# Decoder layer on one core: four row-maxima tiles and one norm step of the third attention change their place in a hand-written order

## The chip, the cores and the metric

The kernel runs on one core of a Trainium2 chip as one launch. The metric is the device time of that launch in microseconds. Before the change the median of 3 runs is 3247.62 us (3247.37 to 3250.29).

## The reference, cut to what matters

A post-norm decoder layer on x (16 x 224 x 512) and a context (16 x 750 x 512), in four parts one after the other: a causal self-attention with low-rank additions to its weights, a second self-attention with biases, a cross-attention of 224 queries on 750 keys per batch, and a feed-forward part (512 to 2048 to 512, then a second one with ternary weights). Each attention has 16 heads of 32. The change touches the third one:

```
Q = split(q_in @ wq + bq, Sq)
K = split(k_in @ wk + bk, Sk)
V = split(v_in @ wv + bv, Sk)
scores = jnp.einsum('bhqd,bhkd->bhqk', Q, K) / HD ** 0.5
probs = jax.nn.softmax(scores, axis=-1)
ctx = jnp.einsum('bhqk,bhkd->bhqd', probs, V)
...
x = _ln(x + h, ln2_g, ln2_b)
```

## The kernel before, in words

Every matmul of the attentions is done in float16 halves (a high and a low part of each operand), so that one product of the reference becomes three. The work of an attention is cut into **units**: one batch and one group of four heads, so four units a batch (g = 0 to 3, called first to fourth unit here) and 64 units an attention. A unit of the cross-attention has these steps; their letters are those of the order tables.

- **q, k0, k1, v0, v1**: projections (L769 on PE). Each ends in one of two banks of PSUM (`ps_proj`). ACT writes the high half (L937, L933), DVE the low half (L981, L979), and with that the bank is free. k0, k1 and v0 are issued on PE in two halves, k0a and k0b and so on; ACT and DVE act after the second.
- **spill, stack**: SP sends the projected Q and K to memory and back into the layout of the scores.
- **M0 to M7, the maxima tiles**: eight per unit (four heads, two tiles of 128 queries). For one tile PE computes 128 x 750 scores with two matmuls of 375 columns (L855), and DVE reduces them to a row maximum (L988, `at_mx_cross`). There is one buffer for such a tile, `ps_qk`, two banks wide, so PE waits before each tile until DVE has reduced the one before it (L851, quoted below).
- **row**: the unit's 8 maxima are transposed on PE (L826), rescaled on ACT (L925, `at_mrow`) and laid by SP as one more row under the queries, so that the scores come out with the maximum already taken off.
- **S0 to S11, the scores**: transposed scores for a pair of key chunks (L890, two matmuls of 224 columns). ACT computes the exponential twice, once to float16 (L944) and once in place (L945), and DVE subtracts the one from the other for the low half (L997, the subtraction). Three banks go round, so PE's Sn waits for the subtraction of S(n-3).
- **V0 to V11, the values**: probabilities times values (L911, eight short matmuls); Vn waits for the subtraction of Sn.
- **E0, E1**: the two evacuations of the values' sums (L951 on ACT; after E1 a reciprocal on DVE, L1002, and two steps on POOL).

At a batch's end come **norm** (L1010, L1014 on DVE, then POOL, L1098 and L1100), **apply** (two DVE operations of 128x512, L1036, then two on POOL, L1106 and L1109) and **store**.

The wait of PE before a maxima tile, in `Attention.tensor`:

```
if self.cross or n == 0 and g == 0 and b == self.b0:
    wait(pe, self.max_done, self.tile(b, g, n))
```

What sets the order is a table written by hand, `ORDERS` (from L58), with one line of tokens for each of the four units of a batch. The function `step` (L1713) turns a line into events, and every engine walks through the same list of events, taking from each what is its own part. So the table fixes the order of each engine's queue, and an engine never takes a later event first. Not every token is of the unit in whose line it stands. With the last tuple of the table, (3, 2, 1, 2), projections, spill and stack in unit u are those of unit u+3, maxima tiles those of unit u+2 (`MAX_AHEAD`), row is that of u+1, and the scores S0 and S1 are those of u+1, while S2 to S11 and all V are of u itself. E1 in unit u is that of u-1. `norm` and `apply` are those of the batch before. The tokens x0, x1, c0 to c5, splitx, splitc, load, loadc, residual, spill, stack and store have no part on PE, ACT or DVE in this attention.

The unit's own work on the three engines is about the same for all four, save that the second unit also has norm and apply.

## Time and profile before

| | |
|---|---|
| median of 3 runs | 3247.62 us |
| profiled execution, its time | 3245.53 us |
| profiled execution, its span | 3243.7 us |
| granted TensorE clock, mean | 0.978 |
| causal attention and second self-attention | up to about 1180 us of the span |
| cross-attention | about 1180 to 2370 us |
| feed-forward part | from about 2370 us |
| busy share of the span | PE 92%, PEld 73%, DVE 79%, ACT 62%, POOL 42% |

PE is the matmul part of TensorE and PEld its weight loads, which run beside the matmuls. DVE is VectorE, ACT ScalarE, POOL GpSimd, SP the queue that issues most transfers. A line such as L855 is a line of the kernel. In a timeline, "x2" counts instructions that were merged, and a bracket at the end gives the idle time before a row and what ended it. The matmuls' ends are modelled; two rows of PE are best compared by their starts.

### The profile page before, as it was taken

To read this page: it belongs to the slowest core of one execution; us is meant where nothing else is said; L and a number is where in the kernel's file an instruction comes from. 1 tells how busy PE (TensorE), PEld (TensorE's weight loads), DVE (VectorE), ACT (ScalarE), POOL (GpSimd) and SP (SyncE) were. 2 spreads that over 40 slices of the span, in tenths; PEclk is the share of its full clock that TensorE was granted. 3 is DMA by queue.
4 is the path that set the end of the run, shared out by engine and by line. 5 is a ranking of instruction groups with operands and counts; after the bars stand their busy time and mean duration, and the time that the engine had idled before them with its cause. 6 is when DMAs were issued, how large, how long until landed. Compare 5 with 4: busy or idle time off the path is not lost.

```text
span 3243.7 us, 87025 instructions
## 1 busy us (share of the span) xinstructions
PE 2988.8 (92%) x34642; PEld 2369.2 (73%) x34642; DVE 2567.3 (79%) x4750; ACT 1995.7 (62%) x4650; POOL 1349.9 (42%) x1273
## 2 busy tenths in 40 slices
PE   7998999988999769999999999999889999999996
PEld 4987888888899647777877778877765565565662
DVE  4776888888899669999999999999846666666666
ACT  2655565667787537777777777877655445344352
POOL 0675632257765544444344344443132232222232
PEclk9999999999999889999999999999899999999997
DMA  4666655456554546655655555554341121211212
GB/s 127 185 206 223 194 180 153 135 159 202 174 162 140 150 118 134 141 141 125 140 137 134 137 135 147 134 129 106 125 152 40 46 53 53 56 45 44 56 40 49
DMA packets 430834, 405.86 MB, mean 125 GB/s; under 512 B 272368, under 2 KB 346240, under 8 KB 429280
## 3 DMA queue, kind: packets, MB, share of 16 engines
q1 hardware_dynamic: 415600, 348.64, 41.0%
q0 software_dynamic: 14576, 51.40, 5.1%
q8 instruction: 277, 4.54, 0.6%
q14 instruction: 125, 1.02, 0.1%
q10 hardware_dynamic: 256, 0.26, 0.0%
HBM read 239.98 MB, written 109.52 MB: 108 GB/s over the span
## 4 chain that ended last, share of the span: by engine, by line
PE 51%; DVE 18%; DMA 13%; ACT 8%; issue 4%; SPq 4%; POOL 1%; ACTq 0%; DVEq 0%; POOLq 0%
PE at_ps L769 22%; PE at_ps L1430 4%; PE at_ps L911 4%; PE at_ps L855 4%; DVE at_mx_cross L988 4%; DVE at_p L997 3%; DMA self_spill<-at_proj 3%; PE at_ps L1444 3%; PE at_ps L890 3%; PE at_ps L1455 3%; PE at_ps L1411 2%; ACT at_ps L945 2%; DVE at_proj L981 2%; DMA at_o_raw<-at_values 2%; PE at_ps L865 2%
## 5 line engine op out<-in xcount | busy, mean ns | idle before, releaser
L944 ACT ACTIVATE at_p<-at_ps 125x448 f16<-125x448 f32 (+2 forms) x1280 | 676.9, 529 | 285.9 <-PE at_ps L890 196.5
L997 DVE TENSOR_TENSOR at_p<-at_ps,at_p 125x448 f16<-125x448 f32 (+2 forms) x1280 | 750.5, 596 | 129.3 <-ACT at_ps L945 119.3
L945 ACT ACTIVATE at_ps<-at_ps 125x448 f32<-125x448 f32 (+2 forms) x1280 | 679.5, 531 | 0.0
L988 DVE TENSOR_REDUCE at_mx_cross<-at_ps 128x1 f32<-128x750 f32 x512 | 476.7, 931 | 26.9 <-PE at_ps L855 24.5
L1070 POOL TENSOR_TENSOR at_o_sum<-at_o_raw 128x256 f32<-128x256 f32 x192 | 121.2, 631 | 782.6 <-ACT at_o_raw L951 782.1
L911 PE MATMUL at_ps<-at_values,at_p 112*128 112x65 f16 (+3 forms) x6656 | 303.3, 185 | 23.4 <-DVE at_p L997 10.5
L1478 ACT ACTIVATE at_masks<-at_ps,at_b_cols 128x256 f32<-128x256 f32 x224 | 106.7, 476 | 336.2 <-PE at_ps L1411 336.1
L992 DVE TENSOR_REDUCE at_mx<-at_ps 112x2 f32<-112x448 f32 (+1 forms) x512 | 303.9, 609 | 10.0 <-PE at_ps L865 7.0
L1411 PE MATMUL at_ps<-at_xt,at_early 128*128 128x256 f16 x1792 | 302.1, 276 | 8.9 <-ACT at_w_first L1479 6.1
L911 PEld LDWEIGHTS at_ps<-at_values,at_p 112*128 112x128 f16 (+1 forms) x6656 | 267.2, 97 | 49.3 <-ACT at_o_raw L951 19.7
L1430 PE MATMUL at_ps<-at_w_second,at_w_first 128*128 128x512 f16 x896 | 283.6, 379 | 0.0
L769 PE MATMUL at_ps<-at_xt,at_w_first 128*128 128x224 f16 x2304 | 254.1, 262 | 3.6 <-DVE at_xt L979 3.0
L769 PE MATMUL at_ps<-at_w_first,at_masks 128*125 128x128 f16 (+1 forms) x2688 | 240.1, 245 | 0.4 <-DVE at_proj L981 0.4
L769 PEld LDWEIGHTS at_ps<-at_xt,at_w_first 128*128 128x128 f16 x2304 | 216.8, 99 | 7.1 <-DVE at_xt L979 3.4
L890 PE MATMUL at_ps<-at_stacks 97*125 97x224 f16 (+1 forms) x1280 | 208.9, 265 | 6.7 <-DMA at_stacks<-at_mrow 6.1
L769 PEld LDWEIGHTS at_ps<-at_w_first,at_masks 128*125 128x125 f16 (+1 forms) x2688 | 179.7, 132 | 40.4 <-issue 2.8
L865 PE MATMUL at_ps<-at_stacks 96*128 96x224 f16 (+2 forms) x1024 | 177.6, 252 | 32.7 <-DMA at_stacks<-self_spill 26.1
L1411 PEld LDWEIGHTS at_ps<-at_xt,at_early 128*128 128x128 f16 x1792 | 175.8, 99 | 37.4 <-ACT at_w_first L1479 6.8
L1411 PE MATMUL at_ps<-at_xt,at_prep 128*128 128x256 f16 x672 | 184.3, 274 | 0.0
L951 ACT COPY at_o_raw<-at_ps 128x260 f32<-128x260 f32 x384 | 147.7, 385 | 55.3 <-PE at_ps L911 55.3
L890 PEld LDWEIGHTS at_ps<-at_stacks 97*125 97x125 f16 (+1 forms) x1280 | 149.9, 136 | 32.1 <-DMA at_stacks<-at_mrow 9.4
L769 PE MATMUL at_ps<-at_xt,at_w_second 128*128 128x224 f16 x1536 | 169.5, 265 | 0.4 <-DVE at_values L979 0.3
(217 smaller groups left out, 6941.7 us busy)
## 6 DMA issues: line engine op xcount, KB each, us to landing
at_x_res<-x SPq DMA_DIRECT2D x124, 256.0 KB, 3.2
cross_spill<-at_proj SPq DMA_DIRECT2D x64, 487.0 KB, 3.2
at_x_rows<-x SPq DMA_DIRECT2D x92, 256.0 KB, 3.1
at_prep<-bit POOLq DMA_DIRECT2D x32, 512.0 KB, 5.5
at_early<-ctx SPq DMA_DIRECT2D x32, 512.0 KB, 5.3
at_stacks<-cross_spill SPq DMA_DIRECT2D x64, 243.5 KB, 3.7
causal_spill<-at_proj SPq DMA_DIRECT2D x64, 224.0 KB, 3.5
at_stacks<-causal_spill SPq DMA_DIRECT2D x128, 112.0 KB, 2.3
```

Of the source, the lines that this page charges most:

```text
L769: mm = pe.matmul(out, left(i, c), right(j, c), start=c == 0 and n == 0, stop=c == DC - 1 and n == 2)
L865: last = pe.matmul(out[:, t, 0:keys[t]], qs[0:96, n, q0:q0 + rows], ks[0:96, n, 0:keys[t]], start=True, stop=not self.causal)
L890: last = pe.matmul(mem.ps_st[0:KC, bank, at:at + T], ks[:, h, c * KC:(c + 1) * KC], qs[:, h, 0:T], start=True, stop=True)
L911: last = pe.matmul(mem.ps_pv[:, t, at_h:at_h + cols], left, vs[:, c, h, 0:cols], start=n % HALF == 0 and c == 0 and t == 0 and k == 0, sto ...
L944: act.activation(mem.p_hi[0:self.KC, n % 4, 0:self.P_COLS], scores, ACT.Exp, scale=EXP_SCALE)
L945: act.activation(scores, scores, ACT.Exp, scale=EXP_SCALE).then_inc(self.exp_done, 1)
L951: act.copy(mem.o_raw[:, g % 2, :, 2 * VW * n:2 * VW * (n + 1)], mem.ps_pv).then_inc(self.pv_evac, 1)
L988: dve.tensor_reduce(self.mx[:, at, t, h:h + 1], mem.ps_qk[:, :, 0:self.KT // 2], AX.XY, ALU.max).then_inc(self.max_done, 1)
L992: dve.tensor_reduce(self.mx[0:rows, at, :, n], mem.ps_qk[0:rows, n % 2, 0:2 * T].rearrange("p (t k) -> p t k", t=2), AX.X, ALU.max).then_i ...
L997: dve.tensor_tensor(mem.p_lo[0:self.KC, n % 4, cols], mem.ps_st[0:self.KC, self.st_bank(b, g, n), cols], mem.p_hi[0:self.KC, n % 4, cols], ...
L1411: last = pe.matmul(out, self.f1[w][quarter][:, c, at:at + P], self.xt[:, x, c, :], start=c == 0 and k == 0, stop=c == DC - 1 and k == 2)
L1430: last = pe.matmul(mem.ps_c[:, t, :], self.ht[:, x, c, t * P:(t + 1) * P], self.f2[w][:, c, :], start=c == 0 and k == 0, stop=c == FC - 1 ...
```

## The change

Only the cross-attention's table changes, and `step` learns one more letter. `L` is like `M`, a maxima tile, but of the unit `MAX_AHEAD - 1` = 1 ahead, not 2.

- Second unit's line: M6 and M7 are gone. M0 stands behind k1b, no longer ahead of it. M1 stands behind S5 (and x0, x1), no longer between V1 and S5. M5 stands behind S11, no longer ahead of it. apply is gone.
- Third unit's line: L6 stands behind E1 and L7 behind V0; these are the tiles that the second unit gave up. M0 moves from behind q to behind k0a, M1 from ahead of S4 to behind k1a, M2 from there to behind V3, M3 from behind V3 to behind S7, M6 from behind V8 to behind V10. M7 is gone. apply stands behind k0b.
- Fourth unit's line: L7 stands behind S2.

The first unit's line is as before. No instruction is added or taken away; the queue of SP has the same order as before.

```diff
--- before.py
+++ after.py
@@ -69,11 +69,11 @@
                (5, 3, 2, 1)),
     "cross": (("c4 E1 S2 k0a V0 V1 M0 k0b V2 M1 S3 q row M2 S4 V3 k1a M3 residual c5 S5 k1b M4 S6 V4 S7 S8 V5 v0a M5 "
                  "E0 S9 v0b V6 S10 spill V7 load M6 splitx S11 S0 V8 v1 S1 stack V9 M7 V10 V11",
-                 "S2 k0a splitc0 E1 S3 k0b norm S4 V0 q k1a M0 k1b V1 M1 spill S5 apply x0 x1 stack V2 V3 V4 M2 "
-                 "S6 S7 V5 row v0a M3 S8 E0 v0b M4 S9 V6 V7 V8 S10 M5 S11 v1 M6 loadc0 S0 V9 V10 V11 M7 S1",
-                 "E1 q M0 S2 S3 V0 c0 splitc1 k0a M1 S4 c1 k0b k1a M2 S5 V1 k1b row V2 S6 V3 M3 V4 S7 S8 v0a V5 M4 E0 "
-                 "S9 v0b V6 M5 S10 spill S11 V7 v1 V8 M6 S0 V9 stack loadc1 V10 S1 V11 M7",
-                 "E1 S2 S3 q V0 c2 V1 row V2 splitc2 c3 M0 S4 k1a M1 loadc2 S5 k1b M2 S6 S7 V3 V4 V5 k0a E0 M3 S8 k0b "
+                 "S2 k0a splitc0 E1 S3 k0b norm S4 V0 q k1a k1b M0 V1 spill S5 x0 x1 M1 stack V2 V3 V4 M2 "
+                 "S6 S7 V5 row v0a M3 S8 E0 v0b M4 S9 V6 V7 V8 S10 S11 M5 v1 loadc0 S0 V9 V10 V11 S1",
+                 "E1 L6 q S2 S3 V0 L7 c0 splitc1 k0a M0 S4 c1 k0b apply k1a M1 S5 V1 k1b row V2 S6 V3 M2 V4 S7 M3 S8 v0a V5 "
+                 "M4 E0 S9 v0b V6 M5 S10 spill S11 V7 v1 V8 S0 V9 stack loadc1 V10 M6 S1 V11",
+                 "E1 S2 L7 S3 q V0 c2 V1 row V2 splitc2 c3 M0 S4 k1a M1 loadc2 S5 k1b M2 S6 S7 V3 V4 V5 k0a E0 M3 S8 k0b "
                  "M4 S9 V6 v0a M5 S10 S11 V7 V8 V9 spill M6 S0 v0b stack S1 V10 v1 store M7 V11"),
                (3, 2, 1, 2)),
 }
@@ -1728,6 +1728,8 @@
                     at, what = resolve(b, g + (0 if n >= layer.AHEAD else 1)), ("scores", n)
                 elif kind == "V":
                     at, what = (layer, b, g), ("values", n)
+                elif kind == "L":
+                    at, what = resolve(b, g + layer.MAX_AHEAD - 1), ("max", n)
                 elif kind == "M":
                     at, what = resolve(b, g + layer.MAX_AHEAD), ("max", n)
                 elif kind == "E":
@@ -1759,7 +1761,7 @@
                     yield at[0], "stack", at[1], at[2], 0
                     yield None, "prep", 0, 0, turn
                     continue
-                if kind in ("E", "S", "M") or token in ("row", "spill", "stack") or token in at[0].UNIT_JOBS:
+                if kind in ("E", "S", "M", "L") or token in ("row", "spill", "stack") or token in at[0].UNIT_JOBS:
                     yield at[0], what[0], at[1], at[2], what[1]
                 else:
                     yield at[0], what[0], at[1], 0 if kind != "V" else g, what[1]
```

The order of DVE's queue in the second unit of a batch, from the subtraction of S4 on. L981 with 224 columns is q, with 375 a half of the keys; L988 is a maxima tile; L1036 is apply. Before:

```order
L997 TENSOR_TENSOR at_p<-at_ps,at_p 125x448
L981 SCALAR_TENSOR_TENSOR at_proj<-at_ps,at_cross_b_cols,at_proj 128x224
L988 TENSOR_REDUCE at_mx_cross<-at_ps 128x1
L981 SCALAR_TENSOR_TENSOR at_proj<-at_ps,at_cross_b_cols,at_proj 128x375
L988 TENSOR_REDUCE at_mx_cross<-at_ps 128x1
L997 TENSOR_TENSOR at_p<-at_ps,at_p 125x448
L1036 TENSOR_SCALAR at_yn<-at_z,at_mv,at_rstd 128x512 x2
L988 TENSOR_REDUCE at_mx_cross<-at_ps 128x1
L997 TENSOR_TENSOR at_p<-at_ps,at_p 125x448 x2
```

Now:

```order
L997 TENSOR_TENSOR at_p<-at_ps,at_p 125x448
L981 SCALAR_TENSOR_TENSOR at_proj<-at_ps,at_cross_b_cols,at_proj 128x224
L981 SCALAR_TENSOR_TENSOR at_proj<-at_ps,at_cross_b_cols,at_proj 128x375
L988 TENSOR_REDUCE at_mx_cross<-at_ps 128x1
L997 TENSOR_TENSOR at_p<-at_ps,at_p 125x448
L988 TENSOR_REDUCE at_mx_cross<-at_ps 128x1 x2
L997 TENSOR_TENSOR at_p<-at_ps,at_p 125x448 x2
L988 TENSOR_REDUCE at_mx_cross<-at_ps 128x1
```

What moved: the low half of k1 now stands ahead of M0, both M1 and M2 stand behind the subtraction of S5, and apply is gone.

The order of DVE's queue in the third unit, from the subtractions of S2 and S3 on. Before (the first L988 is M1, the last M3):

```order
L997 TENSOR_TENSOR at_p<-at_ps,at_p 125x448 x2
L988 TENSOR_REDUCE at_mx_cross<-at_ps 128x1
L997 TENSOR_TENSOR at_p<-at_ps,at_p 125x448
L981 SCALAR_TENSOR_TENSOR at_proj<-at_ps,at_cross_b_cols,at_proj 128x375
L988 TENSOR_REDUCE at_mx_cross<-at_ps 128x1
L997 TENSOR_TENSOR at_p<-at_ps,at_p 125x448
L981 SCALAR_TENSOR_TENSOR at_proj<-at_ps,at_cross_b_cols,at_proj 128x375
L997 TENSOR_TENSOR at_p<-at_ps,at_p 125x448
L988 TENSOR_REDUCE at_mx_cross<-at_ps 128x1
L997 TENSOR_TENSOR at_p<-at_ps,at_p 125x448 x2
L988 TENSOR_REDUCE at_mx_cross<-at_ps 128x1
```

Now (the two L988 of the second row are L7 and M0, then M1, M2, M3):

```order
L997 TENSOR_TENSOR at_p<-at_ps,at_p 125x448 x2
L988 TENSOR_REDUCE at_mx_cross<-at_ps 128x1 x2
L997 TENSOR_TENSOR at_p<-at_ps,at_p 125x448
L981 SCALAR_TENSOR_TENSOR at_proj<-at_ps,at_cross_b_cols,at_proj 128x375
L1036 TENSOR_SCALAR at_yn<-at_z,at_mv,at_rstd 128x512 x2
L988 TENSOR_REDUCE at_mx_cross<-at_ps 128x1
L997 TENSOR_TENSOR at_p<-at_ps,at_p 125x448
L981 SCALAR_TENSOR_TENSOR at_proj<-at_ps,at_cross_b_cols,at_proj 128x375
L997 TENSOR_TENSOR at_p<-at_ps,at_p 125x448
L988 TENSOR_REDUCE at_mx_cross<-at_ps 128x1
L997 TENSOR_TENSOR at_p<-at_ps,at_p 125x448
L988 TENSOR_REDUCE at_mx_cross<-at_ps 128x1
```

What moved: L7 and M0 stand behind the subtraction of S3, M2 behind that of S6 and M3 behind that of S7, and apply stands ahead of M1.

The order of PE's queue in the third unit, from the last matmul of V0 on. L769 with x6 is a half of k0, with x12 k0b and k1a. Before (the two L855 are M1 and M2):

```order
L911 MATMUL at_ps<-at_values,at_p 128x65
L769 MATMUL at_ps<-at_w_second,at_w_first 128x375 x6
L855 MATMUL at_ps<-at_w_first 128x375 x2
L890 MATMUL at_ps<-at_stacks 125x224 x2
L769 MATMUL at_ps<-at_w_second,at_w_first 128x375 x12
L855 MATMUL at_ps<-at_w_first 128x375 x2
```

Now (the L855 are L7, M0 and M1):

```order
L911 MATMUL at_ps<-at_values,at_p 128x65
L855 MATMUL at_ps<-at_stacks 128x375 x2
L769 MATMUL at_ps<-at_w_second,at_w_first 128x375 x6
L855 MATMUL at_ps<-at_w_first 128x375 x2
L890 MATMUL at_ps<-at_stacks 125x224 x2
L769 MATMUL at_ps<-at_w_second,at_w_first 128x375 x12
L855 MATMUL at_ps<-at_w_first 128x375 x2
```

What moved: L7 and M0 now stand with only one half projection, six matmuls, between them.

## Rows read from the trace of the kernel before

**Rows 1.** Windows, one per unit (second, third, fourth, first); columns: window, length, busy times, clock, DMA.

```profile
1511.16:1531.28 20.12, 17.87 (x253) 14.86 (x249) 18.93 (x34) 14.16 (x32) 6.90 (x6) 1.00 0.66 124
1531.28:1549.07 17.79, 17.41 (x249) 14.75 (x247) 16.09 (x26) 15.14 (x34) 7.78 (x6) 1.00 0.44 111
1549.07:1567.22 18.15, 17.80 (x247) 14.49 (x246) 16.64 (x27) 14.76 (x33) 5.47 (x5) 1.00 0.68 133
1567.22:1585.12 17.90, 17.66 (x252) 14.71 (x249) 15.97 (x26) 13.99 (x33) 12.04 (x9) 1.00 0.70 183
```

**Rows 2.** Line L855 within 1230:2310, its idle time by releaser (us, times).

```profile
  DVE at_mx_cross L988: 111.5, 231
```

**Rows 3.** Timeline of PE, second unit; columns: start us, length us, instruction, idle before.

```profile
1516.01 0.49 PE L855 MATMUL at_ps<-at_stacks 96*128 96x375 f16 x2
1516.34 1.12 PE L769 MATMUL at_ps<-at_w_second,at_w_first 128*128 128x375 f16 x6
1517.30 0.39 PE L911 MATMUL at_ps<-at_prep,at_p 125*128 125x33 f16 x8
1518.28 0.49 PE L855 MATMUL at_ps<-at_stacks 96*128 96x375 f16 x2 [0.59 <-DVE at_mx_cross L988]
...
1519.81 0.49 PE L855 MATMUL at_ps<-at_stacks 96*128 96x375 f16 x2 [0.18 <-DVE at_mx_cross L988]
...
1520.70 0.40 PE L911 MATMUL at_ps<-at_prep,at_p 125*128 125x33 f16 x8
...
1526.88 0.49 PE L855 MATMUL at_ps<-at_stacks 96*128 96x375 f16 x2 [0.87 <-DVE at_mx_cross L988]
...
1530.75 0.50 PE L855 MATMUL at_ps<-at_stacks 96*128 96x375 f16 x2 [0.60 <-DVE at_mx_cross L988]
```

**Rows 4.** Timeline of DVE, second unit.

```profile
1517.29 0.93 DVE L988 TENSOR_REDUCE at_mx_cross<-at_ps 128x1 f32<-128x750 f32 x1
1518.14 0.60 DVE L981 SCALAR_TENSOR_TENSOR at_proj<-at_ps,at_cross_b_cols,at_proj 128x375 f16<-128x375 f32 x1
1518.81 0.94 DVE L988 TENSOR_REDUCE at_mx_cross<-at_ps 128x1 f32<-128x750 f32 x1
1520.02 0.62 DVE L997 TENSOR_TENSOR at_p<-at_ps,at_p 125x448 f16<-125x448 f32 x1 [0.27 <-ACT at_ps L945]
1520.56 0.99 DVE L1036 TENSOR_SCALAR at_yn<-at_z,at_mv,at_rstd 128x512 f32<-128x512 f32 x2
```

**Rows 5.** Timeline of PE, third unit.

```profile
1532.76 0.55 PE L890 MATMUL at_ps<-at_stacks 97*125 97x224 f16 x4
...
1539.11 0.38 PE L890 MATMUL at_ps<-at_stacks 97*125 97x224 f16 x2
1539.33 0.39 PE L911 MATMUL at_ps<-at_values,at_p 125*128 125x65 f16 x8
1539.56 0.48 PE L855 MATMUL at_ps<-at_w_first 96*128 96x375 f16 x2
...
1542.13 0.48 PE L855 MATMUL at_ps<-at_w_first 96*128 96x375 f16 x2
...
1548.74 0.49 PE L855 MATMUL at_ps<-at_w_first 96*128 96x375 f16 x2 [0.33 <-DVE at_mx_cross L988]
```

**Rows 6.** Timeline of DVE, third unit.

```profile
1534.39 1.29 DVE L997 TENSOR_TENSOR at_p<-at_ps,at_p 125x448 f16<-125x448 f32 x2
...
1540.55 0.62 DVE L997 TENSOR_TENSOR at_p<-at_ps,at_p 125x448 f16<-125x448 f32 x1 [0.43 <-ACT at_ps L945]
1541.09 0.93 DVE L988 TENSOR_REDUCE at_mx_cross<-at_ps 128x1 f32<-128x750 f32 x1
```

**Rows 7.** Windows of the second self-attention and of the cross-attention.

```profile
700.00:1180.00 480.00, 419.96 (x5837) 382.51 (x5834) 402.22 (x865) 325.78 (x773) 328.27 (x304) 0.96 0.55 162
1480.00:1780.00 300.00, 287.00 (x3985) 237.88 (x3983) 274.16 (x446) 235.49 (x519) 131.24 (x106) 1.00 0.59 136
```

## The prediction

> **What bounds the kernel now.** I read the windows first, cut at the start of each unit of one batch of the cross-attention [rows 1]. The four lengths add up to 73.96 us a batch. The second unit is the longest, 20.12 us against 17.79 to 18.15, and there DVE is busy for 18.93 us, 94% of it. PE does the same matmuls in every unit, so the extra time is lost on it. Then I read one line, L855, the matmuls of the maxima tiles: over 1080 us its rows had 111.5 us of idle time that a DVE reduction ended (weight loads and matmuls counted apart) [rows 2]. Last the timelines show how. PE's queue is in order, and it stops before a maxima tile until the one before is reduced: in the second unit four times [rows 3]. By starts, less the work between them, it loses 0.76 us at the first (a values pair takes 0.22, so from 1517.30 + 0.22 to 1518.28), 0.17 more than the bracket shows, since ends are modelled. The others so read are 0.35, 1.04 and 0.77, and a values pair waits for 0.16 (1519.81 + 0.33 + 0.40 to 1520.70): 3.08 us. That leaves 17.04 us of work in the unit, and by the same work the third unit lost 0.75, the fourth 1.1 and the first 0.85 [rows 1]. DVE in the second unit has norm and apply besides.
>
> So PE's order is the path of the attention, and a stop of PE counts unless a later stop shrinks by it.
>
> **The prices, from rows.** (a) From the start of a reduction to the next tile on PE: 1517.29 to 1518.28, 0.99 us [rows 3, 4]. (b) From a tile's start on PE to its reduction at the earliest: 1518.28 to 1518.81, 0.53. (c) From scores on PE, over ACT's two exponentials, to the subtraction on DVE at the earliest: 1539.11 to 1540.55, 1.44 [rows 5, 6], and 18.61 to 20.02 gives 1.41 by the next start behind the tile at 1518.28 (0.33 for the tile) [rows 3, 4]; I take 1.41. For two scores in a row the second subtraction starts at 1534.39 + 1.29 - 0.62 = 1535.06 for scores at 1532.76, so 2.30 [rows 5, 6]. (d) A subtraction holds DVE for 0.54 before a reduction may start (1540.55 to 1541.09), a reduction 0.85 (1517.29 to 1518.14, its row says 0.93, so 0.08 overlaps), apply 0.99 less the same 0.08, so 0.91 [rows 4]. (e) The low half of a key projection: 1516.34 to 1518.14, 1.80 from its last half's start. (f) PE: tile 0.33, scores 0.20, values 0.22, half of a key projection 0.96 (1516.34 to 1517.30).
>
> DVE's queue is in order too. A tile whose reduction stands behind a subtraction pays (c), (d) and (a) before PE may start the next tile: 1.41 + 0.54 + 0.99 = 2.94 us from the scores. Before, this happens with long work between: S6 at 1539.11, M3's reduction at 1541.09, M4 at 1542.13, with a half of v0 in between [rows 5, 6].
>
> **Part by part.** No instruction is added or removed, so nothing costs by itself.
>
> *Second unit.* M0 goes behind k1b and starts at 1516.97. On DVE its reduction stands behind k1's low half, ready at 1516.01 + 1.80 = 1517.81, and 0.53 long, so it runs at 1518.34 and M1 may start at 19.33. On PE only V1 and S5 lie between, up to 17.72: a stop of 1.6 us where there was one of 0.76. M1 is reduced at 19.33 + 0.53 = 19.86, so M2 starts at 20.85, 1.04 later than before [rows 3]. Of that the wait of 0.16 at the values pair is taken back; M4 is 0.88 late. M4's reduction stands behind v0's low half as before, so M5 keeps its distance and comes at 27.76 for 26.88. Behind it S11 is already done (0.20), M6 and M7 are gone (0.65) and the stop before M7 (0.77). The unit ends at 30.5 for 31.28: **0.75 us less**, of which 0.65 is work that is done one unit later.
>
> *Third unit, start.* Here PE meets S2, S3, V0, L7, k0a, M0, with L7 and M0 behind the subtraction of S3 on DVE. M0 may start 2.30 + 0.54 + 0.99 = 3.83 us after S2, and PE has 0.40 + 0.22 + 0.33 + 0.96 = 1.91 us of work: at least 1.92 lost in both stops. L6 also stands behind the last subtractions of the unit before and the reciprocal, which makes it some 2.1: L7 starts at 1533.6 and M0 at 36.05.
>
> *Third unit, middle.* From M0 on three halves of key projections lie between the tiles, so apply (0.91 on DVE), between k0's low half and M1, is covered: M2 has its release at 40.8 and comes at 41.05. If that cover went, it would cost up to its 0.91. Then S6, V3, M2, V4, S7, M3: M2's reduction stands behind the subtraction of S6, so M3 can't come before S6 + 2.94, and PE has 0.20 + 0.22 + 0.33 + 0.22 + 0.20 = 1.17 of work: 1.77 lost at least, 2.0 with ACT still busy with S6 (row and k1 are ahead of it). M3 at 43.8, M4 at 45.95. Going on to the unit's end, with M6 behind V10: 52.0 where 49.07 was. In sum 2.1 + 2.0 and a third of a microsecond for one more tile, less the 0.75 that the unit lost before (0.50 of it at 1548.74, bracket and 0.17) [rows 1, 5]: **+3.7**.
>
> *Fourth unit.* S0, V9, V10, M6, S1, V11, S2, L7: M6's reduction is behind the subtraction of S0, so L7 waits for S0 + 2.94 against 0.20 + 0.44 + 0.33 + 0.20 + 0.22 + 0.20 = 1.59 of work: 1.35 lost, and 0.33 for the tile itself. DVE has more time to catch up, so I let 0.6 of the 1.1 that this unit lost vanish: **+1.1**. The first unit is as before.
>
> POOL's steps of apply come later with it, behind E1 and the split of c1 in its queue; store stands at the end of the fourth unit, some 25 us on, and SP's order is the same. POOL is busy for 7.8 of 17.79 us in the third unit [rows 1], so I count this at nothing; without that room the store would hold SP's queue.
>
> **The sum.** -0.75 + 3.7 + 1.1 = 4.05 us, taken as 4.0 a batch. 15 batches have it whole; in the last one the feed-forward matmuls stand between, and I give it 1. So 15 x 4.0 + 1 = 61 us on the profiled execution's 3245.53: 3306.5. The median of the runs is 2.1 us above that execution, so 3308.6 in its terms. For 1.2 us a batch either way, the forecast's own range is 3290 to 3327.
>
> The Trainium skill (Perfetto Trace Analysis, Identifying the Most-Contended Engine) would have one take the occupancy of VectorE as the measure and relieve the engine that is fullest. By that rule the second unit is DVE's and the change takes 2.6 us of DVE's work out of it, which leads to rival B; the sum would be negative. The rows of PE speak against it: what PE waits for is the place of one reduction in a queue.
>
> **Rivals.**
>
> *A, the stops are only the bare minimum and DVE catches up everywhere.* Lost: 1.92 + 1.77 + 1.35 = 5.04. Gained: all 3.08 of the second unit, the 0.75 of the third and 0.6 of the fourth. +0.6 a batch, with the last one 10 us: 3258; with all 1.1 of the fourth +0.1 a batch and 3249. For it: stops on one resource do shrink each other. Against: M1 of the second unit gets a longer one by the same arithmetic.
>
> *B, balance of work decides: faster.* The second unit gives up two reductions (1.7) and apply (0.9): DVE 18.93 - 2.6 = 16.3, PE 17.04 - 0.65 = 16.4, so the unit would run in about 17.4, as the others do with 1 us over their work: -2.7. The third gets DVE 16.09 + 0.85 + 0.91 = 17.85, so 18.7: +0.9. The fourth +0.35. In all -1.45 a batch, 22 us: 3226. It decides if PE's wait is met without the subtraction ahead, that is, if the stop before M3 in the third unit stays under 0.5 us. Against it are rows 5 and 6, where the chain from S6 took its full 2.97 (1539.11 to the reduction's 1541.09 + 0.99).
>
> *C, the clock.* The cross-attention runs at a granted clock of 1.00 with PE busy for 96% of the time; the second self-attention at 0.96 with 87% [rows 7]. With 4 us more of stops a batch PE is busy for about 91%. Halfway, at 0.98, its 70.7 us of work take 1.4 longer: 21 us more, 3330. The Trainium skill (TensorE: Matmul & The Clock Gate, A second HAM failure mode: psum-queue depth-cycling) says that short idle times between groups of matmuls can bring the clock down again and again. By that rule C is what happens; in this trace the second unit had 3 us of stops and 1.00.
>
> *D, no difference that shows.* Only if the events came out in another order than I read; the lists of both kernels speak against that.
>
> **Chances.** Forecast 0.74, A 0.10, B 0.05, C 0.09, D 0.02. The range is 3283 to 3335: the forecast with its bounds and C; A, B and D lie outside, 0.17. A change of 0.2% is about what a measurement of this kernel can tell from none. Faster 0.05 (B), same 0.02 (D), slower 0.93.
>
> **What would show it.** A batch of about 78 us, with units of 19.4, 21.5, 19.2 and 17.9. In the third unit idle time of PE before L855 right behind the half of k0 (1.2), before L7 (0.9) and at M3 (2.0); in the fourth 1.35 at its first tile; in the second 1.6 at M1 and none before the gone M7. The idle time of L855 by DVE well above 111.5 us. I am wrong if M3's stop is under 0.5 us, if the second unit comes out near 17.4, or if the granted clock leaves 1.00.

## Result and profile after the change

| | before | after |
|---|---|---|
| median of the runs | 3247.49 us (4 runs, 3241.56 to 3250.29) | 3334.65 us (4 runs, 3323.32 to 3339.37) |
| profiled execution, its time and span | 3245.53 us, 3243.7 us | 3339.37 us, 3337.6 us |
| granted TensorE clock, mean | 0.978 | 0.971 |

After to before is 1.0273, 95% interval 1.0254 to 1.0292: slower by 2.7%. The forecast was 3308.6 with a range up to 3335.0. The direction is right. The size is not: 1.0273 x 3247.5 is 3336, just past the end of a range whose last part was rival C's, and the 61 us of the forecast became 89.

The windows of the four units of one batch come first, cut where those of before were cut [rows 1]. The columns are length, busy us of PE, PEld, DVE, ACT and POOL with their instructions, granted clock, DMA share, GB/s; the first line is the second unit.

```profile
1534.56:1553.93 19.37, 16.93 (x249) 14.29 (x246) 16.89 (x30) 13.60 (x32) 2.18 (x4) 1.00 0.64 130
1553.93:1575.99 22.06, 18.06 (x250) 14.95 (x248) 18.59 (x29) 14.88 (x33) 12.47 (x8) 1.00 0.44 100
1575.99:1595.65 19.66, 18.11 (x254) 14.80 (x251) 18.07 (x28) 15.75 (x35) 5.46 (x5) 1.00 0.44 103
1595.65:1613.60 17.95, 17.66 (x253) 14.71 (x249) 15.98 (x26) 14.00 (x33) 12.04 (x9) 1.00 0.72 185
sum 79.04, PE 70.77 PEld 58.75 DVE 69.53 ACT 58.23 POOL 32.16; mean PE 17.69 PEld 14.69 DVE 17.38 ACT 14.56 POOL 8.04
```

The batch is 79.04 us long, and was 73.96. The second unit is shorter by the 0.75 us that were forecast, to the hundredth. The third has grown by 4.27 and the fourth by 1.51. PE and ACT are busy for what they were; DVE is busy for about 2 us more, of which 1.1 are one long apply (below).

PE's stops of that batch, its rows at L855 with idle time (start, length, engine, line, form; the bracket is the idle time and what ended it):

```profile
1542.69 0.49 PE L855 MATMUL at_ps<-at_stacks 96*128 96x375 f16 x2 [1.39 <-DVE at_mx_cross L988]
1544.22 0.50 PE L855 MATMUL at_ps<-at_stacks 96*128 96x375 f16 x2 [0.37 <-DVE at_mx_cross L988]
...
1551.12 0.49 PE L855 MATMUL at_ps<-at_stacks 96*128 96x375 f16 x2 [0.69 <-DVE at_mx_cross L988]
...
1556.82 0.49 PE L855 MATMUL at_ps<-at_stacks 96*128 96x375 f16 x2 [0.65 <-DVE at_mx_cross L988]
1559.52 0.48 PE L855 MATMUL at_ps<-at_w_first 96*128 96x375 f16 x2 [1.25 <-DVE at_mx_cross L988]
...
1565.32 0.50 PE L855 MATMUL at_ps<-at_w_first 96*128 96x375 f16 x2 [0.61 <-DVE at_mx_cross L988]
1567.74 0.49 PE L855 MATMUL at_ps<-at_w_first 96*128 96x375 f16 x2 [1.49 <-DVE at_mx_cross L988]
...
1577.65 0.49 PE L855 MATMUL at_ps<-at_w_first 96*128 96x375 f16 x2 [1.28 <-DVE at_mx_cross L988]
```

They are M1, M2 and M5 of the second unit, L7, M0, M2 and M3 of the third, and L7 of the fourth. By starts, each stop is 0.16 to 0.17 longer than its bracket: 1.56, 0.53, 0.85, then 0.81, 1.42, 0.78, 1.65, then 1.44. With the small ones the batch has 10.6 us of stops, where by the same reading it had 5.6. One of them, 0.78 at M2 of the third unit (1565.32), is not in the forecast. The line's summary for the stretch of [rows 2] says the same for all batches:

```profile
  DVE at_mx_cross L988: 233.5, 281
```

It was 111.5 us, 231 times.

Two things were not foreseen. The first is on DVE at apply in the third unit; the rows are DVE's and then POOL's of the same microseconds.

```profile
1561.80 0.61 DVE L981 SCALAR_TENSOR_TENSOR at_proj<-at_ps,at_cross_b_cols,at_proj 128x375 f16<-128x375 f32 x1
1562.33 2.08 DVE L1036 TENSOR_SCALAR at_yn<-at_z,at_mv,at_rstd 128x512 f32<-128x512 f32 x2
1564.34 0.93 DVE L988 TENSOR_REDUCE at_mx_cross<-at_ps 128x1 f32<-128x750 f32 x1
```

```profile
1560.41 1.05 POOL L1062 TENSOR_SCALAR at_prep<-at_early 128x1024 f16<-128x1024 f32 x1
1561.54 2.14 POOL L1064 TENSOR_TENSOR at_prep<-at_early,at_prep 128x1024 f16<-128x1024 f32 x1
1564.49 2.35 POOL L1106 TENSOR_TENSOR at_yn<-at_yn,at_gain 128x1024 f32<-128x1024 f32 x1 [0.82 <-DVE at_yn L1036]
```

The two operations of apply hold DVE for 2.08 us, not 0.99 [rows 4], while POOL is in L1064, the last step of the split of c1, until 1563.68. M1's reduction starts 1.1 us late, at 1564.34, and with (a) of the forecast, 0.99, that gives M2's start at 1565.32. L1036 in the 13 or 14 batches between 1300 and 2350 us, first before and then after (count, then min/median/max ns; after, one operation of a pair is long in 12 of the 13 batches):

```profile
L1036 DVE TENSOR_SCALAR at_yn<-at_z,at_mv,at_rstd x28: 536/539/546, 1371.8 to 2341.4; 128x512 f32<-128x512 f32 x28
```

```profile
L1036 DVE TENSOR_SCALAR at_yn<-at_z,at_mv,at_rstd x26: 533/538/1630, 1322.2 to 2289.3; 128x512 f32<-128x512 f32 x26
```

The second is the clock. These windows cover 13 batches, from one start of L1010 (norm) to the one 13 batches on, before and after:

```profile
1292.30:2255.80 963.50, 919.78 (x12795) 764.05 (x12793) 879.12 (x1432) 754.47 (x1665) 409.87 (x332) 1.00 0.58 134
```

```profile
1296.60:2346.20 1049.60, 942.55 (x12795) 783.48 (x12793) 903.85 (x1432) 757.90 (x1665) 409.61 (x332) 0.98 0.52 123
```

Before, not one of the 13 batches has a stretch at the lower of the two clock levels (1.2 GHz); after, 8 of them have, 51.2 us together. They are 13 stretches. Six begin just behind M2's start in the second unit, right behind the stops of M1 and M2, and six within 1 us of M3's start in the third. The one that is left begins at the stops of L7 and M0 in the third unit, and two windows next to each other show it:

```profile
1398.37:1401.78 3.41, 3.23 (x12) 1.86 (x13) 1.60 (x3) 1.13 (x3) 3.24 (x3) 0.50 0.00 0
1394.37:1398.37 4.00, 2.28 (x23) 1.41 (x20) 3.74 (x7) 2.36 (x6) 3.62 (x4) 1.00 0.02 4
```

PE was busy for 2.28 of the 4.00 us ahead of its fall. The Trainium skill (TensorE: Matmul & The Clock Gate, A second HAM failure mode: psum-queue depth-cycling) describes this kind of loss, a clock that swings when TensorE is briefly idle between groups of matmuls; the trace agrees, with 0.98 for 1.00 over the 13 batches.

So of the 93.9 us by which the span grew, 86.1 lie in these 13 batches, 4.3 ahead of them (1296.6 against 1292.3) and 3.5 behind.

### The profile page after: what moved, and what is told of

Read it like the earlier page. It is cut to its first block, busy times and chain, and to the rows that moved or that the text cites. A ratio compares the mean times of both kernels' runs of the same rounds, so it can differ in the third digit from the quotient of the medians.

```text
span 3337.6 us, 87025 instructions
## 1 busy us (share of the span) xinstructions
PE 3015.6 (90%) x34642; PEld 2390.5 (72%) x34642; DVE 2596.1 (78%) x4750; ACT 2000.7 (60%) x4650; POOL 1351.0 (40%) x1273
## 4 chain that ended last, share of the span: by engine, by line
PE 55%; DVE 17%; DMA 12%; ACT 7%; issue 4%; SPq 3%; POOL 2%; ACTq 0%; POOLq 0%; DVEq 0%
PE at_ps L769 24%; PE at_ps L911 5%; DVE at_mx_cross L988 4%; PE at_ps L855 4%; PE at_ps L1430 4%; PE at_ps L890 4%; PE at_ps L1455 3%; PE at_ps L1444 3%; DVE at_p L997 3%; DMA self_spill<-at_proj 2%; PE at_ps L1411 2%; ACT at_ps L945 2%; DMA at_o_raw<-at_values 2%; PE at_ps L865 2%; DMA at_stacks<-cross_spill 2%
## 5 line engine op out<-in xcount | busy, mean ns | idle before, releaser
L997 DVE TENSOR_TENSOR at_p<-at_ps,at_p 125x448 f16<-125x448 f32 (+2 forms) x1280 | 754.8, 596 | 139.3 <-ACT at_ps L945 127.0
L988 DVE TENSOR_REDUCE at_mx_cross<-at_ps 128x1 f32<-128x750 f32 x512 | 476.4, 931 | 70.2 <-PE at_ps L855 68.3
L992 DVE TENSOR_REDUCE at_mx<-at_ps 112x2 f32<-112x448 f32 (+1 forms) x512 | 303.9, 609 | 13.0 <-PE at_ps L865 10.6
L769 PE MATMUL at_ps<-at_xt,at_w_first 128*128 128x224 f16 x2304 | 252.8, 261 | 3.6 <-DVE at_xt L979 3.0
L769 PE MATMUL at_ps<-at_w_first,at_masks 128*125 128x128 f16 (+1 forms) x2688 | 249.4, 251 | 0.4 <-DVE at_proj L981 0.4
L769 PEld LDWEIGHTS at_ps<-at_xt,at_w_first 128*128 128x128 f16 x2304 | 216.1, 98 | 8.4 <-DVE at_xt L979 3.4
L769 PEld LDWEIGHTS at_ps<-at_w_first,at_masks 128*125 128x125 f16 (+1 forms) x2688 | 189.8, 139 | 41.5 <-issue 2.9
L855 PE MATMUL at_ps<-at_stacks 96*128 96x375 f16 x512 | 126.4, 328 | 53.9 <-DVE at_mx_cross L988 47.1
L769 PE MATMUL at_ps<-at_xt,at_w_second 128*128 128x224 f16 x1536 | 172.9, 268 | 0.5 <-DVE at_values L979 0.5
```

The costliest lines, as they stand in the source:

```text
L769: mm = pe.matmul(out, left(i, c), right(j, c), start=c == 0 and n == 0, stop=c == DC - 1 and n == 2)
L855: last = pe.matmul(mem.ps_qk[:, half, 0:KT // 2], qs[0:96, h, TILES[t]:TILES[t] + P], ks[0:96, h, half * KT // 2:(half + 1) * KT // 2], st ...
L988: dve.tensor_reduce(self.mx[:, at, t, h:h + 1], mem.ps_qk[:, :, 0:self.KT // 2], AX.XY, ALU.max).then_inc(self.max_done, 1)
L992: dve.tensor_reduce(self.mx[0:rows, at, :, n], mem.ps_qk[0:rows, n % 2, 0:2 * T].rearrange("p (t k) -> p t k", t=2), AX.X, ALU.max).then_i ...
L997: dve.tensor_tensor(mem.p_lo[0:self.KC, n % 4, cols], mem.ps_st[0:self.KC, self.st_bank(b, g, n), cols], mem.p_hi[0:self.KC, n % 4, cols], ...
```

## Experiments

Every run is told by its ratio to the kernel before, and by numbers of its trace, above all two: the **clean batch**, the median length of those of the 13 batches that have no half-clock stretch, and the microseconds at half clock in the 13. The trace is of one execution of each kernel, and the half-clock time differs between executions (the mean clock of the whole kernel is 0.970 to 0.974 over the four runs of after). All edits but a1's are of the cross-attention's table; in the short diffs only the tokens around the edit are shown and the rest of a line stands as it was.

| run | ratio, 95% interval | clean batch | shortest clean | 13 batches | at half clock |
|---|---|---|---|---|---|
| before | 1 | 73.96 (13) | 73.64 | 963.5 | 0 |
| after | 1.0273 [1.0254, 1.0292] | 79.04 (5) | 78.61 | 1049.6 | 51.2 |
| a1_filler | 1.0212 [1.0189, 1.0236] | 79.08 (13) | 78.61 | 1030.2 | 0 |
| a2_split_later | 1.0240 [1.0210, 1.0271] | 78.44 (5) | 77.93 | 1041.9 | 47.8 |
| a3_split_m2 | 1.0202 [1.0178, 1.0226] | 77.75 (5) | 77.22 | 1026.0 | 34.1 |
| a4_split_l7 | 1.0219 [1.0189, 1.0250] | 77.74 (4) | 77.43 | 1023.2 | 34.1 |
| b1_second_back | 1.0264 [1.0232, 1.0295] | 78.66 (6) | 77.96 | 1038.0 | 34.1 |
| b4_all_back | 1.0102 [1.0085, 1.0119] | 76.44 (12) | 76.05 | 999.7 | 3.4 |
| b2_second_alone | 1.0110 [1.0083, 1.0138] | 75.63 (8) | 75.50 | 994.1 | 17.1 |
| b3_apply_alone | 1.0036 [1.0019, 1.0053] | 74.64 (12) | 74.32 | 975.1 | 3.4 |
| c1_norm_first | 1.0044 [1.0027, 1.0060] | 75.13 (13) | 74.79 | 979.7 | 0 |
| c2_norm_end_first | 1.0038 [1.0023, 1.0054] | 74.93 (13) | 74.58 | 977.3 | 0 |
| c3_norm_behind_m0 | 1.0044 [1.0026, 1.0062] | 74.32 (10) | 74.06 | 975.4 | 10.2 |
| c4_norm_m2 | 1.0009 [0.9992, 1.0026] | 74.42 (13) | 73.81 | 967.9 | 0 |

In brackets behind the clean batch is how many of the 13 are clean. Clean batches of one kernel differ too, in before from 73.64 to 75.08 us. Most of that is a wait of PE for a transfer of the first unit's stack, which is absent in some batches and 1.04 us in the bracket of this one of before:

```profile
1421.55 0.49 PE L855 MATMUL at_ps<-at_stacks 96*128 96x375 f16 x2 [1.04 <-DMA at_stacks<-cross_spill]
```

So a few tenths between two medians can be this wait. The shortest clean batch has little or none of it (0.28 us by starts in a4_split_l7).

### The clock: a1_filler

The changed kernel, with needless matmuls put where PE would stop. Nothing of the computation is left out.

```diff
+            fill, at = {(3, 1): (14, 6), (3, 2): (4, 6), (0, 0): (12, 4), (0, 2): (7, 7), (0, 3): (14, 8)}.get((g, n), (0, 0))
+            if self.cross and fill and not (b == self.b0 and g == 0):
...
+                for _ in range(fill):
+                    pe.matmul(mem.ps_st[0:KC, self.st_bank(bs, gs, at), 0:T], self.ks(bs, gs)[:, at // 3, 0:KC],
+                              self.qs(bs, gs)[:, at // 3, 0:T], start=True, stop=True)
             if self.cross or n == 0 and g == 0 and b == self.b0:
                 wait(pe, self.max_done, self.tile(b, g, n))
```

> The changed kernel, with needless matmuls that fill PE's stops: the scores matmul of the next pair, 0.093 us each, is issued ahead of five maxima tiles a batch into the bank which that pair overwrites anyway (14 ahead of M1 and 4 ahead of M2 in the second unit, 12 ahead of M0, 7 ahead of M2, 14 ahead of M3 in the third). They take 4.8 us a batch and fit into the stops of 1.56, 0.53, 1.42, 0.78 and 1.65 us. Theory 'stops plus clock' (the surplus over the stops is half-clock stretches that the stops bring on): batches stay at the clean length of 79.0 us, the stretches at half clock between 1290 and 2420 us of the span go from 16 to nearly none, and the whole is some 20 to 24 us faster than the changed kernel (ratio to before about 1.020 instead of 1.027) although PE does more. Rival 'all of it is waiting on queues, the clock is by the way': no change or slower, by up to 5 us a batch if the fillers do not fit.

Measured: 1.0212, and all 13 batches clean. The window over the 13 batches:

```profile
1293.40:2323.60 1030.20, 984.46 (x13458) 826.74 (x13456) 904.65 (x1432) 757.84 (x1665) 409.77 (x332) 1.00 0.53 126
```

PE does 663 matmuls more and the kernel is faster. The clean batch is what it was, 79.08, so the filler brought no tile forward; it took the half clock away, and with it 19.4 us of the 13 batches, 0.38 us for each of the 51.2. The intervals of this run and of after don't meet. That the clock falls because PE stands still, and what it costs, is shown.

### What the stops are made of: a2, a3, a4

a2_split_later is the changed kernel with the split of c1 (on POOL) behind apply. a3_split_m2 is a2 with M2 of the third unit ahead of S6, and a4_split_l7 is a2 with L7 of the third unit ahead of S2.

```diff
-... L7 c0 splitc1 k0a M0 S4 c1 k0b apply k1a M1 ...
+... L7 c0 k0a M0 S4 c1 k0b apply splitc1 k1a M1 ...
```

```diff
-... k1b row V2 S6 V3 M2 V4 S7 M3 S8 ...
+... k1b row V2 M2 S6 V3 V4 S7 M3 S8 ...
```

```diff
-... E1 L6 q S2 S3 V0 L7 c0 ...
+... E1 L6 q L7 S2 S3 V0 c0 ...
```

> The changed kernel with splitc1 (three POOL steps) moved behind apply in the third unit. Theory 'POOL holds DVE off': of DVE's two apply operations the one that meets POOL's L1064 (two inputs, 2.14 us) took 1.63 us instead of 0.54; with POOL's split behind apply both take 0.54, the stop of 0.78 us before M2 in the third unit goes, and M3, which hangs on S6, comes 0.54 earlier: a clean batch of 78.5 us for 79.0, some 8 us less in all. Rival 'apply is slow because of its place in DVE's queue or because of ACT': no change.

> As the one with splitc1 behind apply, and M2 in the third unit ahead of S6 instead of behind V3 (M2 S6 V3 V4 S7 M3). Theory 'place in DVE's queue': M2 is then reduced ahead of S6's subtraction; M3 stops PE for 0.7 us instead of 1.65 and M4 comes 1.5 us earlier than in the changed kernel: a clean batch of 77.5 us, some 22 us less than the changed kernel plus what the clock gives back. Rival 'DVE has too much work in the third unit, wherever the tiles stand': the stop moves to the next tile and the batch stays at 78.5.

> As the one with splitc1 behind apply, and L7 in the third unit ahead of S2 instead of behind V0. Theory 'place in DVE's queue': L7 now stops PE longer (1.45 us for 0.81, it follows L6 with only q between), but M0 has its release in time (0 for 1.42): M0 comes 0.7 us earlier, a clean batch of 77.8 us. Rival 'amount of work': as the one with splitc1 alone, 78.5.

a2 gave 78.44, and every apply is short again:

```profile
L1036 DVE TENSOR_SCALAR at_yn<-at_z,at_mv,at_rstd x26: 535/538/544, 1327.3 to 2290.3; 128x512 f32<-128x512 f32 x26
```

So apply is long where POOL's split runs beside it, and that costs 0.6 us a batch. It is less than M2's stop of 0.78, which is gone, because M3's stop grew by 0.11 and a wait for a transfer by 0.13. The Trainium skill (SBUF — State Buffer, SBUF: two separate sides) says that VectorE and GpSimd share one pair of ports, which one of them holds alone for a whole instruction; the rows fit in part, with 0.54 us without and up to 1.63 with L1064 beside it. The long operation, the first of the pair, ends 0.28 us behind L1064 (1563.96 and 1563.68), which is less than a whole operation of 0.54 behind it. That the ports are the cause was not tested by itself.

a3 gave 77.75 and a4 77.74, 0.7 each. In a3 M2's reduction no longer stands behind the subtraction of S6, and M3's stop goes from 1.76 in a2 to 0.71, with 0.13 new ones at M2 and M4. In a4 L7's reduction no longer stands behind the subtractions of S2 and S3: of the stops of 0.81 and 1.42 one of 1.42 is left. Both are the mechanism of the forecast, a reduction behind a subtraction, each taken away at one place, and both came as expected.

### The second unit and apply: b1 to b4

b1_second_back is the changed kernel with M0, M1 and M5 of the second unit back in their places; b2_second_alone is the kernel before with only these three moved; b3_apply_alone is the kernel before with only apply moved to the third unit, behind k0b. b4_all_back has the edits of a3, a4 and b1 together.

```diff
-S2 k0a splitc0 E1 S3 k0b norm S4 V0 q k1a k1b M0 V1 spill S5 x0 x1 M1 stack V2 V3 V4 M2 ...
+S2 k0a splitc0 E1 S3 k0b norm S4 V0 q k1a M0 k1b V1 M1 spill S5 x0 x1 stack V2 V3 V4 M2 ...
-... V8 S10 S11 M5 v1 ...
+... V8 S10 M5 S11 v1 ...
```

> The changed kernel with M0, M1 and M5 of the second unit back in the places of before (M0 ahead of k1b, M1 ahead of S5, M5 ahead of S11); M6, M7 and apply stay moved. Theory 'place in DVE's queue': M1 and M2 stop PE as before the change, the second unit takes 18.7 us for 19.37, a clean batch 78.4 for 79.04, some 10 us less in all. Rival 'the reordering of the second unit is what the change gains by, its cost is the third unit alone': the clean batch gets longer, 79.5 or more.

> The kernel before with only M0, M1 and M5 of the second unit moved (behind k1b, behind S5, behind S11); all eight tiles and apply stay in the second unit. Theory 'place in DVE's queue': the first tiles come 1.8 us late (k1's low half and apply now stand ahead of reductions), M6 gets a stop behind S11's subtraction: a clean batch of 75.9 us for 73.96, some 28 us slower than before. Rival 'this part is harmless or helps': 73.5 to 74.2.

> The kernel before with apply alone moved to the third unit, behind k0b. Theory 'POOL holds DVE off': apply meets POOL's split of c1 there (L1060, L1062, L1064 run from 1536.6 to 1541.0 of the profile before, k0's low half ends at 1537.5), so one or both of its operations take over 1 us, and M2's reduction behind it comes up to 1 us late; in the second unit nothing is gained, since no stop of PE hangs on apply. A clean batch of 74.3 us (73.9 to 74.9). Rival 'DVE's work is the bound of the second unit': 73.0, the 0.9 us of apply gone from the longest unit.

> The changed kernel with four of its edits bent back at once: the split of c1 behind apply, M2 ahead of S6 in the third unit, L7 ahead of S2 in the fourth, and M0, M1, M5 of the second unit where they stood before. What is left of the change is that M6 and M7 of the second unit are done in the third and one tile on in the fourth, M0 and M1 of the third unit stand later, and apply is in the third. If the terms add up as the single runs had them (79.0 - 0.6 - 0.7 - 0.1 - 0.5, or -1.0 by the best batches of the run with the second unit back): 77.0 us a batch without half clock, no apply operation over 0.6 us, and with some 25 us of half clock in the attention about 3300 us, 1.016. If the second unit's gain and the third unit's exclude each other, 77.7 us and 3312 us.

b2 gave 75.63, 1.7 us over before, and 1.0110. Part of what it costs comes from the clock, though it has only 7.2 us of stops in the batch read. Two of them, 1.56 and 1.29, stand 2.3 us apart, and all five half-clock stretches of its trace begin within 0.7 us behind the start of the second tile. b4 has 8.4 us in the batch read and hardly any half clock (3.4 us against 17.1; the mean clocks of all its runs are 0.977 to 0.982, b2's 0.973 to 0.977). So the sum of the stops does not rank these two, and neither does PE's busy share, 0.92 in b4 and 0.93 in b2. Long stops close together are not the only case. Nine of a4's ten stretches begin at one stop of 1.71 us, c3's three at one of 1.69 or 2.04, b3's at one of 2.61, b4's at one of 1.95, each with no other stop over 0.3 us in the 8 us ahead. What share length and spacing have was not tested.

b3 gave 74.64, 0.7 over before. Its rival, a gain from relieving the fullest unit, was 73.0. Here too apply meets POOL's split:

```profile
L1036 DVE TENSOR_SCALAR at_yn<-at_z,at_mv,at_rstd x28: 534/902/2335, 1321.7 to 2297.2; 128x512 f32<-128x512 f32 x28
```

But in 12 of these 14 batches the long operation stands beside another step of it, L1062. DVE, then POOL:

```profile
1546.04 1.72 DVE L1036 TENSOR_SCALAR at_yn<-at_z,at_mv,at_rstd 128x512 f32<-128x512 f32 x2
1546.24 1.23 POOL L1062 TENSOR_SCALAR at_prep<-at_early 128x1024 f16<-128x1024 f32 x1
```

The second of the pair takes 1.26 us and ends at 1547.75, again 0.28 behind POOL's step, and that step itself is 1.23 long where it is 1.05 elsewhere. In one batch both are long, the second beside L1064 with 2.34. M2 then stops for 2.61 us, and the trace's only half-clock stretch begins there.

b1 is not told apart from after by its time (1.0264). Its six clean batches fall into two kinds, three of 78.0 to 78.2 and three of 79.2 to 80.3, and the median lies between them. The second kind has longer waits for transfers, which no theory had; this is one for the first unit's stack:

```profile
1853.57 0.49 PE L855 MATMUL at_ps<-at_stacks 96*128 96x375 f16 x2 [1.65 <-DMA at_stacks<-cross_spill]
```

Why this transfer is late in some batches and not in others, in before too, stays open. By the shortest clean batches the three moves are worth 0.65 us (78.61 to 77.96), as was expected.

b4 gave 76.44 and 1.0102. Its expectation has two slips: L7 is the third unit's, and its term is 0.7 by a4, not 0.1. With 79.04 - 0.60 - 0.69 - 0.70 and 0.4 to 0.65 for b1 the terms add up to 76.4 to 76.65, so they hold together within 0.2. The half-clock time fell with them, from 51.2 to 3.4 us. What b4 still has over before, 2.5 us, lies in what it shares with the change: the two tiles passed on, M0 and M1 of the third unit later, and apply. Its largest stops there are 1.41 at L7 of the third unit and 1.32 at L7 of the fourth; the three were not parted by a run.

### Can the second unit be relieved at all? c1 to c4

The change took reductions out of the second unit. These four take the kernel before and move norm, 1.5 us of DVE, away from M0's reduction instead.

```diff
-... load M6 splitx S11 ...
+... load M6 norm splitx S11 ...
```

```diff
-... V9 M7 V10 V11
+... V9 M7 V10 V11 norm
```

```diff
-... k0b norm S4 V0 q k1a M0 k1b V1 M1 ...
+... k0b S4 V0 q k1a M0 norm k1b V1 M1 ...
```

```diff
-... k0b norm S4 V0 q k1a M0 k1b V1 M1 spill S5 apply x0 x1 stack V2 V3 V4 M2
+... k0b S4 V0 q k1a M0 k1b V1 M1 spill S5 x0 x1 stack V2 V3 V4 M2 norm
-... v1 M6 loadc0 ...
+... v1 M6 apply loadc0 ...
```

> The kernel before with norm alone moved out of the second unit, to the first unit behind M6 (and splitx). Theory 'place in DVE's queue': norm's 1.55 us on DVE stood right ahead of q's low half and M0's reduction, and made M1 stop PE for 0.76 us and M2 for 0.35; in the first unit it stands where the next tile is 2.7 us of PE's work away and the one after M7 more than 5. The stops at M1 and M2 shrink to under 0.3 in sum: a clean batch of 73.1 us for 73.96, some 13 us faster than before. Rival 'amount of DVE's work': the first unit gets longer by what the second gets shorter, no change.

> The kernel before with norm as the last thing of the first unit, behind V11, and not behind k0b in the second. On VectorE that is ahead of E1's reciprocal and of the subtraction of S2, and VectorE has no idle time in that stretch, so the same amount of work stands ahead of M0's reduction at 1517.29: the stop before M1 (0.76 in the second unit) should stay, and the batch be 73.9 us, within 0.3. GpSimd's splits are issued ahead of it as before, so no apply operation is long. If norm itself is what makes M0's reduction late, wherever it stands, nothing changes either; if the place behind k0b is what costs (norm waits for nothing there, but the low half of the keys and S3's subtraction are close), the batch gains up to 0.7 and the time is 3237 us. If norm now delays the subtractions of S1 and S2 and PE stops for the values, it is up to 1 us longer a batch, 3262 us.

> The kernel before with norm behind M0 in the second unit, not behind k0b. By the queue arithmetic: M0's reduction runs when its scores are there, 1516.54, so the stop of 0.76 before M1 goes. But norm's 1.5 us now stand between it and k1's low half, so M1's reduction comes at 19.4 (it was 18.81), M2 may start at 20.4 (it was 19.81), and everything behind is 0.6 later: 74.5 us a batch, 15 x 0.55 = 8 us, 1.0025. If only the stop counts that was seen in the trace of before, the batch is 73.2 and the time 3236 us.

> The kernel before with norm behind M2 and apply behind M6, both still in the second unit. By the same arithmetic: M0's reduction at 1516.54, M1's at 18.3, M2's at 20.6, so PE loses no 0.76 before M1 and is 0.7 to 0.8 ahead at the first half of v0; norm then delays M3's reduction (24.2 for 24.3 its end, no loss), and v0's low half comes 0.5 earlier than before, and M5 with it. Apply behind M6 delays M7's reduction by 0.4 of its 0.9, which takes most of it back at M0 of the third unit. GpSimd's part of apply then runs into E1's steps there and puts them some 3 us off, which I count at nothing. 73.4 to 73.9 us a batch, 0 to 8 us less in all: 3240 to 3248 us, 0.9975 to 1.000. If GpSimd's late steps or norm in front of the subtractions cost PE a stop, 74.5 us and 1.0025.

**c1** missed: 75.13, not 73.1. The stop before M1 went as expected, but others came. DVE and PE around norm, and M2:

```profile
1513.25 1.27 DVE L1010 BATCH_NORM_STATS2 at_stats<-at_z 128x6 f32<-128x512 f32 x2
1514.63 0.25 DVE L1014 BATCH_NORM_AGGREGATE at_mv<-at_stats 128x2 f32<-128x6 f32 x2
1514.79 1.12 DVE L997 TENSOR_TENSOR at_p<-at_ps,at_p 125x448 f16<-125x448 f32 x2
```

```profile
1515.44 0.40 PE L911 MATMUL at_ps<-at_w_second,at_p 125*128 125x33 f16 x8 [1.14 <-DVE at_p L997]
1524.14 0.49 PE L855 MATMUL at_ps<-at_stacks 96*128 96x375 f16 x2 [0.73 <-DVE at_mx_cross L988]
```

```profile
1522.63 0.61 DVE L981 SCALAR_TENSOR_TENSOR at_proj<-at_ps,at_cross_b_cols,at_proj 128x375 f16<-128x375 f32 x1 [0.63 <-ACT at_proj L937]
1523.15 0.93 DVE L988 TENSOR_REDUCE at_mx_cross<-at_ps 128x1 f32<-128x750 f32 x1
```

Norm holds two subtractions, and a values pair of PE waits for them, 1.3 us by starts. M2 stops for 0.89, because M1's reduction stands behind the low half of k1 on DVE, and that waits 0.63 us for ACT's high half. This follows from prices (e), (b) and (a) of the forecast, k1b's start at 1520.86 + 1.80 + 0.53 + 0.99 = 1524.18, and the same 0.89 stands at M2 in c2 and c4. So with norm out of the way the first stops of this unit, 1.27 us in before, could shrink by 0.4 and not by the 0.8 that was expected. And POOL, which now takes norm's small steps ahead of the split of x, comes late with the splits:

```profile
1514.96 0.22 POOL L1098 TENSOR_SCALAR at_ve<-at_mv 128x2 f32<-128x2 f32 x1 [13.86 <-DVE at_mv L1014]
...
1522.79 2.12 POOL L1064 TENSOR_TENSOR at_prep<-at_early,at_prep 128x1024 f16<-128x1024 f32 x1
```

It had idled for 13.86 us in front of that step, and L1064 now ends at 1524.91, beside apply (1524.53, 1.44 us for the two). Behind apply PE loses only 0.19 us, at M3.

**c2** missed too: 74.93 for 73.9, where only its last rival had the sign. The stop before M1, which was to stay, is gone, but PE stops at a place that none of the three cases named:

```profile
1526.79 1.13 PE L769 MATMUL at_ps<-at_w_second,at_w_first 128*128 128x375 f16 x6 [1.14 <-DVE at_proj L981]
```

The first half of k1 waits for a PSUM bank, and so for the low half of k0, which before stood ahead of norm. Another stop, the 0.89 at M2, follows.

**c3** was a test of the arithmetic, and hit. M0's reduction starts at 1516.57 in this run (16.54 expected), M1's at 1519.47 (19.4), and M2 on PE at 1520.45 (20.4). DVE, then PE:

```profile
1516.57 0.94 DVE L988 TENSOR_REDUCE at_mx_cross<-at_ps 128x1 f32<-128x750 f32 x1 [0.34 <-PE at_ps L855]
1517.43 1.28 DVE L1010 BATCH_NORM_STATS2 at_stats<-at_z 128x6 f32<-128x512 f32 x2
...
1519.47 0.93 DVE L988 TENSOR_REDUCE at_mx_cross<-at_ps 128x1 f32<-128x750 f32 x1
```

```profile
1520.45 0.49 PE L855 MATMUL at_ps<-at_stacks 96*128 96x375 f16 x2 [1.53 <-DVE at_mx_cross L988]
```

A stop of 0.76 at M1 has become one of 1.69 at M2, by starts. The batch is 74.32 (74.5 expected). The 10.2 us of half clock cost another 4 us, and the two together make about 1.003 of the 1.0044; the trace is of the fastest of the ten runs, 9 us under their median, so the others probably have more half clock.

**c4** is at 1.0009 [0.9992, 1.0026], not told apart from before. 74.42 a batch lies by the unfavourable case of its expectation, but part of it is the wait for the transfer: the shortest are 73.81 and 73.64, and the time lies between the two cases. M1's stop is gone, and M2 has one of 0.89 instead. None of the twelve is faster than the kernel before.

## Why the prediction was right and where it failed

**The path was named rightly.** PE's queue, DVE's queue and the wait for one buffer give the stops. The stops forecast were 1.6 at M1 (measured 1.56), 0.9 at L7 (0.81), 1.2 at M0 (1.42), 2.0 at M3 (1.65) and 1.35 at the fourth unit's L7 (1.44). The second unit was forecast at -0.75 and came at -0.75. Rival B (balance of work, faster) is refuted twice: M3's stop is not under 0.5, and b3, which does nothing but take apply off the fullest unit, is slower.

**Step "Third unit, middle", the words "is covered: M2 has its release at 40.8".** This failed. Apply was costed at 0.91 from [rows 4], taken beside an idle POOL. Next to L1064 it holds DVE for 2.08. M2 stopped for 0.78, and the unit came at 22.06 for the 21.5 forecast: the stops of this unit were 4.66 in sum and the forecast had 2.1 + 2.0. The sentence behind it, POOL's part "I count this at nothing", looked only at whether POOL had room. What mattered was what it ran at that moment. The term is worth 0.6 us a batch by a2, 8 us in 13 batches.

**Step "Fourth unit", the words "I let 0.6 of the 1.1 that this unit lost vanish".** By starts the small stops of this unit were 1.1 in sum and 0.8 are left: 0.3 vanished. With 1.44 for L7's stop and 0.33 for the tile the unit grew by 1.5 and not by 1.1.

**The sum, 4.0 a batch.** With these two it is 5.1 (79.08 - 73.96), so 66.7 us in 13 batches, where the forecast had 52.

**Step "The sum", no term for the clock; rival C at 0.09.** This is the larger failure. C said that with 4 us more of stops the clock falls, and gave 21 us at 0.98. After measured 0.98 and a1_filler 19.4 us. C was not another way the change could go, but a term to be added to the forecast: the stops that the forecast itself put in were its cause. I had weighed the kernel before, 3 us of stops in a unit and a clock of 1.00, as evidence against, though its longest stop for a reduction was 1.04 and the change put stops of 0.5 to 1.65 at eight places. That C's 21 us came so close to 19.4 is in part luck: its 0.98 was taken halfway between two other stretches and not worked out. The forecast's own sign of being wrong, that the granted clock leaves 1.00, came true. The Trainium skill's rule, cited there beside C, was on the right side.

Added up on the profiled execution: 61 forecast, 14.7 by the sum of the stops (66.7 - 52), 19.4 by the clock, which makes 95, where the span grew by 93.9.

**What was only partly settled.** Which of the moves costs what depends on the rest. Moving M0, M1 and M5 costs 1.7 us a batch by itself (b2), but undoing it in the changed kernel gave back 0.4 by the medians and 0.65 by the shortest batches (b1), and 0.6 by the medians with the others undone (b4). These three are not told apart. The 1.7 is another matter: in b2 apply, M6 and M7 stand in that unit too. The price of one edit depends on what else stands in the queue.

## What to carry to other kernels

An in-order queue is not relieved by taking work out of its fullest stretch: find which one operation the path waits for, and what stands in front of it in its queue, since whatever is moved away will stand in front of another. Before an operation moves, read what every engine that shares something with it runs at its new place, not how busy it is there. And if a forecast puts long stops on TensorE, longer or closer than those of the trace that it starts from, add the clock to the same sum, and don't keep it as a rival.

## What the hardware showed that was not expected

- VectorE's scale-and-shift of 128 x 512 (L1036) takes 0.54 us; beside a two-input step of GpSimd of 2.14 us (L1064) one of the pair took up to 1.63 us, in another run 2.34, and beside a one-input step (L1062) 1.26. In each of these rows it ended 0.28 us behind GpSimd's step, and L1062 itself took 1.23 us for 1.05. The subtraction L997 and the low half L981 of VectorE, which read PSUM, kept their 0.62 and 0.61 beside the same step.
- Stops cost twice. With the stops filled the 13 batches had a clock of 1.00 and took 1030.2 us; at a mean of 0.98 they took 1049.6. Each microsecond at the lower level cost about 0.38.
- The kernel with 663 matmuls more that nobody needs was faster by 0.6% (1.0212 for 1.0273), with the intervals apart.
- The sum of the stops does not tell the half-clock time: 7.2 us a batch with two long ones 2.3 us apart had 17.1 us of it in 13 batches (b2), 8.4 us a batch had 3.4 (b4), and in a4 nine stretches began at a single stop of 1.71.
